# Decoder layer on one core: in the attention turns, two of four query products move ahead of the fourth tile's scores

## The chip, the cores and the metric

One core of a Trainium2 chip runs the whole program. The metric is the device time of one execution in microseconds (us); the median of three runs of the kernel before is 2265.24 us.

## The reference, cut to what matters

One decoder layer on x of shape (4, 2048, 512), in float32: a recurrent (S5) part, a cross attention and a feed-forward part, each behind a layer norm and added to x. The change touches only the stage of the cross attention:

```
x = x + S5(layernorm(x))
Q = layernorm(x) @ Wq.T            16 heads of 32; K, V from a context of 77 rows per batch
attn = softmax(Q K^T / sqrt(32))
x = x + (attn V) @ Wo.T
x = x + FFN(layernorm(x))
```

## The kernel before, in words

The program is written by hand, engine by engine: each engine has its own list of instructions, in order, and semaphores tie the lists together. The 8192 tokens are 16 groups (`NG`) of 512, each of `T` = 4 tiles of 128 tokens. The stage of the cross attention is a software pipeline of 18 turns (`attn_loop`, L419). Each engine has one body, called once a turn: `attn_pe` (L1925, TensorE), `attn_act` (L1052, ScalarE), `attn_dve` (L1440, VectorE) and `norm` (L852, GpSimd). In turn g, `has(d)` asks whether group g+d exists. A turn works on the scores of group g, on the queries of group g+1, on the values and half of the projection of group g-1 and on the other half of the projection of group g-2; group g+2 gets its layer-norm statistics (`spread2`, L1350).

A tile t of group g goes this way. `scores(t)` (L1938) is 48 matmuls of 32 rows into PSUM banks 0 to 3, and sets `s_done`. `shift(t)` on VectorE (L1474) takes the maxima and subtracts one half of them. `exp(t)` on ScalarE (L1079) is eight exponentials with sums and one large one. `sums(t)` on VectorE (L1487) ends in the reciprocal `rinv`. `norm` on GpSimd multiplies it in (L866). `turn_p(t, d)` on TensorE (L1960) transposes the result, in three slots. Tiles 2 and 3 are transposed only in the next turn, as `turn_p(2, -1)` and `turn_p(3, -1)`.

TensorE's results other than scores go through PSUM banks 4 to 7, by numbered slots: 28 a turn, slot n in bank 4 + n % 4 (P_SLOT to Q_SLOT, from L345). A slot is written by TensorE, copied by ScalarE rounded to its high part (`hi_p`, `hi_x`, `hi_v`, `hi_q`; L1059), and VectorE then writes the low part (`lo_p`, `lo_x`, `lo_v`, `lo_q`; L1314); the slots of `project` are added to x by `residual` (L1468) on VectorE alone. `bank(n)` (L1928) waits for VectorE to have finished the slot four before, and `scores(0)` waits for all slots of the turn before, since it reads the queries that `lo_q(3)` ends. All products are done in three passes (high by high, high by low, low by high), in `split3` (L442). A query product (`query`) is 12 matmuls of 512 columns, four make the next group's queries, into slots 24 to 27. They are written to `qh` and `ql`, which `scores` of the present group reads: no copy may start before `scores(3)` is done.

The order of a steady turn on TensorE is: `turn_p(2, -1)`, `scores(0)`, `project(2, -2)`, `turn_p(3, -1)`, `project(3, -2)`, `scores(1)`, four `values` with `turn_x(0)` and `turn_x(1)` between, `turn_p(0, 0)`, `scores(2)`, `turn_x(2)`, `project(0, -1)`, `turn_x(3)`, `project(1, -1)`, `turn_p(1, 0)`, `scores(3)`, four query products (L2058, L2059).

VectorE and ScalarE also prepare the feed-forward weights inside the turns, one block n a turn: `mix_weights(n)` (VectorE, L1403), `high_weights(n)` (ScalarE, L1039, L1041), then `low_weights(n, 0)` and `low_weights(n, 1)` (VectorE, L1413). These go from one SBUF tile to another. The sync engine's queue stores the block and loads the next (`store_wc`, L634; `load_wc`, L625), and in turns 2 to 13 then stores and loads groups of x (`turn`, L620). It waits for `low_weights(14, 1)` and, after that, for the last query product of turn 14 before it loads the first two groups for the feed-forward part (`load_x2`, L660, L675), whose statistics VectorE takes in turn 15 (`spread3`) and turn 16.

Turn 1 differs: it mixes block 1 late (`mix_weights(1)`), `high_weights(1)` stands behind `hi_q(0)`, and all four statistics of `spread2` come between the query copies. Turn 15 has no queries. Turn 0 has a list of its own in each body and returns early.

Of the kernel before, what the change touches and what calls it, by code (L numbers as in the profile page):

```python
# [20 lines left out]
def decoder_layer(nc, x, ctxT, log_dt, log_re, lam_im, vt, vinv, wqT, wkT, wvT, woT, wexpT, bexp, upbias,  # L21
# [13 lines left out]
    KC = D // P  # L35
# [18 lines left out]
    T = GT // P  # L54
    NG = NB * S // GT
# [225 lines left out]
    with ExitStack() as ctx:  # L281
# [633 lines left out]
        def _(act):  # L915
# [123 lines left out]
            def high_weights(n):  # L1039
                act.wait_ge(wc_ready, n + 1)  # L1040
                A(wc_h[:, :, :], wc_s[:, :, :], ACT.Copy).then_inc(wc_hi, 1)  # L1041
# [10 lines left out]
            def attn_act(g, has):  # L1052
                his.start()
                def hi(out, n):
                    act.wait_ge(pe_slot, SLOTS * g + n + 1)
                    bank = ps[:, 4 + n % 4, :]
                    if len(out.shape) == 3:
                        bank = bank[0:out.shape[0]].rearrange("p (j n) -> p j n", j=4)
                    his.done(A(out, bank, ACT.Copy), hi_slot(g, n))  # L1059

                def hi_p(t, d, qs=range(3)):
                    if has(d):
                        for q in qs:
                            part = (pth[:, 0:KC], pth[:, KC:2 * KC], pt2[0:KT])[q]
                            hi(part[:, :, t * P:(t + 1) * P], P_SLOT[t] + q)

                def hi_x(c):
                    if has(1):
                        hi(xt2h[:, c, :], x_slot(g, c))

                def hi_v(f):
                    if has(-1):
                        hi(aoh[:, f, :], V_SLOT[f])

                def hi_q(o):
                    if has(1):
                        hi(qh[:, o, :], q_slot(g, o))

                def exp(t):  # L1079
                    if has(0):  # L1080
                        act.wait_ge(top_ready, T * g + t + 1)
                        for h in range(HB, HPC):
                            for f in range(KC):
                                at, j = h * KC + f, f * HPC + h
                                e = A(es[t % 2][:, f, h * L:(h + 1) * L], ps[:, h, f * LP:f * LP + L], ACT.Exp,  # L1085
                                      bias=rmax[:, t % 2, at:at + 1], accum_out=rsum[:, t % 2, j:j + 1])
                        e.then_inc(exp_ps, 1)
                        act.wait_ge(e_ready, T * g + t + 1)
                        e = es[t % 2][:, :, 0:HB * L]
                        A(e, e, ACT.Exp).then_inc(exp_done, 1)  # L1090

                if g == 0:
                    exp(0)
                    for c in range(KC):
                        hi_x(c)
                    exp(1)
                    act.wait_ge(upb_ready, 1)
                    for i, out in enumerate(stage_out):
                        act.wait_ge(out, stage_turns(PIECES, i))
                    act.wait_ge(p_zero, 1)  # L1100
                    hi_p(0, 0)
                    exp(2)
                    hi_q(0)
                    hi_q(1)
                    hi_p(1, 0)
                    exp(3)
                    hi_q(2)
                    hi_q(3)
                    return
                hi_p(2, -1)  # L1110
                if g == 1:
                    act.wait_ge(wo_loaded, 16)
                    A(woh[:, :, :], wo_raw[:, :, :], ACT.Copy).then_inc(wo_hi, 1)
                if g == NG:
                    apply3(0)
                    for i in range(4):
                        raw_x(0, i, i, FIRST_TURN[i])
                exp(0)
                hi_p(3, -1)
                if has(1):  # L1120
                    apply2(g + 1)
                if g == NG:
                    act.wait_ge(x2_stored, 16 * (NG - 2))
                    act.wait_ge(wc_stored, 32 * NG)
                    hi_x3(0, B11)
                hi_v(0)
                hi_x(0)
                if g == 1:
                    high_weights(0)
                if g == NG:  # L1130
                    apply3(1, 0, 2)
                exp(1)
                hi_v(1)
                hi_x(1)
                if g == NG:
                    apply3(1, 2, T)
                hi_v(2)
                hi_v(3)
                if g == NG:
                    hi_x3(0, B21)  # L1140
                    for i in range(4, 8):
                        raw_x(0, i, i - 4, FIRST_TURN[i])
                    load_table(ACT.Gelu)
                    for o in FIRST_ORDER[2:]:
                        hi_x3(0, o)
                hi_p(0, 0)
                hi_x(2)
                if 2 <= g < NG:
                    high_weights(g)
                exp(2)  # L1150
                hi_x(3)
                hi_p(1, 0)
                exp(3)
                for o in range(KC):
                    hi_q(o)
                    if g == 1 and o == 0:
                        high_weights(1)

            attn_loop(act, attn_act)

            def gelu(p, c, q, i, chunk, src=None):
# [62 lines left out]
        def _(dve):  # L1224
# [125 lines left out]
            def spread2(g, tiles):  # L1350
                if tiles[0] == 0:
                    dve.wait_ge(x1_loaded, 16 * g + 16)
                ins = spread(x1[:, g % 4], tiles)
                if tiles[-1] == T - 1:
                    ins.then_inc(ln_step, 1)
# [84 lines left out]
            def attn_dve(g, has):  # L1440
# [8 lines left out]
                def lo_p(t, d):  # L1449
                    if has(d):  # L1450
                        for q, part, high in ((0, ptl[:, 0:KC], pth[:, 0:KC]), (1, ptl[:, KC:2 * KC], pth[:, KC:2 * KC]),
                                              (2, pt2[KB:KB + KT], pt2[0:KT])):
                            tok = slice(t * P, (t + 1) * P)
                            lo(part[:, :, tok], high[:, :, tok], P_SLOT[t] + q)
# [9 lines left out]
                def lo_q(o):  # L1464
                    if has(1):
                        lo(ql[:, o, :], qh[:, o, :], q_slot(g, o))
# [7 lines left out]
                def shift(t):  # L1474
                    if not has(0):
                        return
                    n = T * g + t
                    sc = ps[:, 0:HPC, 0:KC * LP].rearrange("p h (f k) -> p h f k", k=LP)[:, :, :, 0:L]
                    mx = rmax[:, t % 2, :].rearrange("p (h f) -> p h f", f=KC)
                    dve.wait_ge(s_done, n + 1)  # L1480
                    V.tensor_reduce(mx[:, HB:], sc[:, HB:], AX.X, ALU.max, negate=True).then_inc(top_ready, 1)  # L1481
                    V.tensor_reduce(mx[:, 0:HB], sc[:, 0:HB], AX.X, ALU.max).then_inc(max_step, 1)
                    dve.wait_ge(max_step, n + 1)
                    V.tensor_tensor(es[t % 2][:, :, 0:HB * L].rearrange("p f (h k) -> p h f k", k=L), sc[:, 0:HB],
                                    mx[:, 0:HB].unsqueeze(3).broadcast_to([P, HB, KC, L]), ALU.subtract).then_inc(e_ready, 1)
# [99 lines left out]
                if g == NG - 1:  # L1585
                    shift(3)
                lo_p(1, 0)
                if not (g == NG - 1):
                    shift(3)
                if g == 1:  # L1590
                    mix_weights(g)
                if has(2) and g > 1:
                    spread2(g + 2, range(0, 3))
                lo_q(0)
                if 0 <= g < NG - 1:
                    low_weights(g, 0)
                sums(3)
                if 0 <= g < NG - 1:
                    low_weights(g, 1)
                lo_q(1)  # L1600
                if has(2):
                    spread2(g + 2, range(3 if g > 1 else 0, T))
                lo_q(2)
                lo_q(3)

            attn_loop(dve, attn_dve)

# [145 lines left out]
        def _(pe):  # L1753
# [171 lines left out]
            def attn_pe(g, has):  # L1925
# [77 lines left out]
                def turn_q(os):  # L2003
                    if has(1):
                        pe.wait_ge(dve_slot, SLOTS * g + x_slot(g, 3) + 1)
                        for o in os:
                            slots.done(query(bank(q_slot(g, o)), o), q_slot(g, o))
# [47 lines left out]
                turn_x(3)  # L2055
                project(1, -1)
                turn_p(1, 0)
                scores(3)  # L2058
                turn_q(range(KC))  # L2059

            attn_loop(pe, attn_pe)

# [151 lines left out]
```

## Time and profile before

| what | value |
|---|---|
| runs | 2263.72, 2265.24, 2268.49 us; median 2265.24 |
| the profiled execution | 2265.3 us, its span on the core 2263.5 us |
| busy, share of the span | PE 98%, DVE 75%, ACT 54%, POOL 21% |
| attention turns 1 to 15 | from 297 us to about 945 us of the span |
| one steady turn | 43.66 us (562.70 to 606.36, start of `scores(0)`) |

PE is TensorE, PEld its weight loads, DVE VectorE, ACT ScalarE, POOL GpSimd, SPq the queue of the sync engine. Times in rows are microseconds from the span's start. An engine starts its next instruction some 0.1 us before the printed end of the last, so work in a row is best counted from start to start.

### The profile page before, as it was taken

Reading aid. Unit: us, or ns where it says so; the run is one execution under the profiler, and the core shown is the slowest. Engines: PE = TensorE matmul, PEld = TensorE weight load, DVE = VectorE, ACT = ScalarE, POOL = GpSimd, SP = SyncE. Lnnn points to the kernel's source line nnn. Section 1 sums busy time; section 2 is a strip of 40 time slices with the busy share of each in tenths; the row PEclk is TensorE's granted clock in tenths of the full one; section 3 lists DMA queues with packets and bytes.
Section 4 is the critical chain, followed back from the end, with each engine's and each line's share of the span. In section 5 each row is a group of like instructions: output and inputs, shape, how many; then the busy total and the mean of one; then the engine's idle time right before and its main releaser. Section 6 shows DMA issues by size and latency. Waiting matters only on the chain.

```text
span 2263.5 us, 41277 instructions
## 1 busy us (share of the span) xinstructions
PE 2218.5 (98%) x15960; PEld 1943.2 (86%) x15960; DVE 1701.5 (75%) x2854; ACT 1231.5 (54%) x2735; POOL 467.4 (21%) x578
## 2 busy tenths in 40 slices
PE   8899889999999999999999999999999999999999
PEld 7678777888888888778989989989989989889899
DVE  6666688888888888857947858758769668579467
ACT  3556566666766666645535536446446356355343
POOL 3531222322223222300020200300300300300203
PEclk8999999999999999999999999999999999999999
DMA  9999613323332331466676686786676676766765
GB/s 319 329 320 319 226 66 122 124 86 112 109 110 86 117 124 62 146 238 206 212 263 184 215 269 174 220 268 195 204 267 208 211 245 207 240 214 209 229 188 194
DMA packets 202091, 443.35 MB, mean 196 GB/s; under 512 B 32442, under 2 KB 70586, under 8 KB 200362
## 3 DMA queue, kind: packets, MB, share of 16 engines
q1 hardware_dynamic: 201898, 440.72, 60.2%
q8 instruction: 128, 2.10, 0.4%
q14 instruction: 65, 0.53, 0.1%
HBM read 341.66 MB, written 99.01 MB: 195 GB/s over the span
## 4 chain that ended last, share of the span: by engine, by line
PE 87%; ACT 5%; DVE 5%; DMA 2%; issue 1%; SPq 0%; POOL 0%; DVEq 0%; POOLq 0%; ACTq 0%
PE ps L442 69%; PE ps L1989 5%; PE ps L1957 4%; PE ps L1968 2%; ACT es L1085 2%; DMA yg<-in_wcon 1%; PE ps L1920 1%; PE ps L1877 1%; ACT wc_h L1041 1%; PE ps L1808 1%; DMA x_scratch<-xa 1%; PE ps L1859 1%; DVE rsum L1492 1%; ACT es L1090 1%; PE ps L1872 1%
## 5 line engine op out<-in xcount | busy, mean ns | idle before, releaser
L442 PE MATMUL ps<-ring,gh 128*128 128x256 f32 x3584 | 652.8, 284 | 0.1
L442 PEld LDWEIGHTS ps<-ring,gh 128*128 128x128 f32 x3584 | 558.2, 192 | 2.1 <-DVE gl L1314 1.5
L442 PE MATMUL ps<-xth,ring 128*128 128x512 f32 x1792 | 553.1, 389 | 0.0
L442 PE MATMUL ps<-ring,gl 128*128 128x256 f32 x1792 | 506.8, 283 | 0.0
L442 PEld LDWEIGHTS ps<-xth,ring 128*128 128x128 f32 x1792 | 336.4, 188 | 69.7
L1182 ACT ACTIVATE gh<-G 128x512 fp32r<-128x512 f32 x384 | 239.2, 629 | 218.6 <-PE ps L442 218.2
L442 PE MATMUL ps<-xtl,ring 128*128 128x512 f32 x896 | 348.6, 389 | 0.0
L442 PEld LDWEIGHTS ps<-ring,gl 128*128 128x128 f32 x1792 | 343.5, 192 | 0.0
L1314 DVE TENSOR_TENSOR gl<-G,gh 128x512 fp32r<-128x512 f32 x384 | 276.5, 732 | 51.4 <-ACT gh L1182 50.3
L866 POOL TENSOR_TENSOR es<-es,rinv 128x308 f32<-128x308 f32 x256 | 180.5, 736 | 388.8 <-DVE rinv L1496 388.8
L1165 ACT ACTIVATE G<-G,up_b 128x512 f32<-128x512 f32 x192 | 138.9, 723 | 222.0 <-DVE G L1608 222.0
L1608 DVE TENSOR_TENSOR U<-ps,U 128x512 f32<-128x512 f32 (+1 forms) x167 | 136.2, 815 | 163.4 <-PE ps L442 160.8
L1608 DVE TENSOR_TENSOR G<-ps,U 128x512 f32<-128x512 f32 x192 | 132.8, 692 | 113.9 <-PE ps L442 112.3
L756 POOL TENSOR_TENSOR rstd<-var_e,mhalf 128x4 f32<-128x4 f32 x48 | 50.5, 1051 | 745.5 <-DVE var_e L1295 745.5
L442 PEld LDWEIGHTS ps<-xtl,ring 128*128 128x128 f32 x896 | 168.2, 188 | 34.6
L1085 ACT ACTIVATE es<-ps,rmax 128x77 f32<-128x77 f32 x512 | 158.3, 341 | 69.6 <-DVE rmax L1481 69.6
L895 POOL TENSOR_TENSOR X<-X,U 128x256 f32<-128x256 f32 x64 | 72.2, 1158 | 472.7 <-DVE U L1608 472.7
L1165 ACT ACTIVATE G<-ps,up_b 128x512 f32<-128x512 f32 x64 | 44.2, 690 | 135.9 <-PE ps L442 135.9
L1085 ACT ACTIVATION_READ_ACCUMULATOR es<-ps,rmax 128x1 f32 x512 | 113.8, 222 | 0.0
L884 POOL TENSOR_TENSOR X<-X,ob 128x512 f32<-128x512 f32 x64 | 86.4, 1382 | 126.6 <-DMA X<-x_scratch 112.8
L442 PE MATMUL ps<-woh,aoh 128*128 128x512 f32 x256 | 106.9, 418 | 2.4 <-DVE x L1472 1.4
L1968 PE MATMUL ps<-ident,es 128*128 128x128 f32 (+1 forms) x768 | 99.2, 276 | 6.7 <-DVE xt2l L1314 2.2
(234 smaller groups left out, 4394.0 us busy)
## 6 DMA issues: line engine op xcount, KB each, us to landing
ring<-wup_scratch SPq DMA_DIRECT2D x224, 512.0 KB, 3.8
ring<-wdn_scratch SPq DMA_DIRECT2D x224, 512.0 KB, 3.6
X<-x_scratch SPq DMA_DIRECT2D x32, 1024.0 KB, 9.0
xa<-in_x SPq DMA_DIRECT2D x16, 1024.0 KB, 6.6
x_scratch<-xa SPq DMA_DIRECT2D x16, 1024.0 KB, 10.6
x<-x_scratch SPq DMA_DIRECT2D x16, 1024.0 KB, 5.6
x_scratch<-x SPq DMA_DIRECT2D x16, 1024.0 KB, 4.3
out_x<-X SPq DMA_DIRECT2D x15, 1024.0 KB, 6.4
```

Of the source, the lines that this page charges most:

```text
L442: mm = pe.matmul(bank, a, b, start=first and i == 0, stop=last and i == n - 1, skip_group_check=go_on)
L866: mul = nc.gpsimd.tensor_tensor(e[:, f], e[:, f], r[:, f].unsqueeze(2).broadcast_to([P, HPC, L]), ALU.mult)
L884: x = tt(X[:, i * T + t, :], X[:, i * T + t, :], ob[:, :], ALU.add)
L895: ins = tt(x, x, U[:, u + t // 2, t % 2 * HW:(t % 2 + 1) * HW], ALU.add)
L1085: e = A(es[t % 2][:, f, h * L:(h + 1) * L], ps[:, h, f * LP:f * LP + L], ACT.Exp, bias=rmax[:, t % 2, at:at + 1], accum_out=rsum[:, t % 2, ...
L1165: A(dst, dst if src is None else src, ACT.Gelu, bias=up_b[:, chunk:chunk + 1]).then_inc(gelu_done, 1)
L1182: A(gh[e % GR][:, :], src, ACT.Copy).then_inc(g_hi, 1)
L1314: sub = lambda o, a, b: V.tensor_tensor(o, a, b.bitcast(F32), ALU.subtract)
L1608: add = lambda o, a, b: V.tensor_tensor(o, a, b, ALU.add)
L1957: mm = pe.matmul(ps[:, h, cols], q[at, f, tok], k[at, b, f, :], start=(i == 0), stop=(i == 2))
L1968: mm = pe.transpose(b[0:keys.shape[1], j * P:(j + 1) * P], keys, ident[:, :])
L1989: mm = pe.matmul(b[0:VW[c]], v[:, f, V_AT[c]:V_AT[c + 1]], pt, start=(i == 0), stop=(i == len(passes) - 1))
```

## The change

On TensorE, query products 0 and 1 stand ahead of `scores(3)`, products 2 and 3 behind it. ScalarE waits for `scores(3)` to be done, copies queries 0 and 1, and only then does `exp(3)`; in turn 1, `high_weights(1)` comes before `hi_q(2)`. VectorE takes three statistics ahead of `shift(3)`, and `sums(3)` goes from behind `lo_q(0)` to behind `lo_q(3)`; the two parts of `low_weights` are spaced out between the query copies, and in turn 1 go to the very end.

```
@@ attn_act
                 exp(2)
                 hi_x(3)
                 hi_p(1, 0)
+                if has(1):
+                    act.wait_ge(s_done, T * g + T)
+                hi_q(0)
+                hi_q(1)
                 exp(3)
-                for o in range(KC):
-                    hi_q(o)
-                    if g == 1 and o == 0:
-                        high_weights(1)
+                if g == 1:
+                    high_weights(1)
+                hi_q(2)
+                hi_q(3)
@@ attn_dve
                 lo_p(1, 0)
+                if has(2) and g > 1:
+                    spread2(g + 2, range(0, 3))
                 if not (g == NG - 1):
                     shift(3)
+                lo_q(0)
+                lo_q(1)
                 if g == 1:
                     mix_weights(g)
-                if has(2) and g > 1:
-                    spread2(g + 2, range(0, 3))
-                lo_q(0)
-                if 0 <= g < NG - 1:
+                if 2 <= g < NG - 1:
                     low_weights(g, 0)
-                sums(3)
-                if 0 <= g < NG - 1:
+                lo_q(2)
+                if 2 <= g < NG - 1:
                     low_weights(g, 1)
-                lo_q(1)
                 if has(2):
                     spread2(g + 2, range(3 if g > 1 else 0, T))
-                lo_q(2)
                 lo_q(3)
+                sums(3)
+                if g == 1:
+                    low_weights(g, 0)
+                    low_weights(g, 1)
@@ attn_pe
                 turn_p(1, 0)
+                turn_q(range(2))
                 scores(3)
-                turn_q(range(KC))
+                turn_q(range(2, KC))
```

## Rows read from the trace of the kernel before

**Rows 1.** Chain of waits, 590 to 640 us: start, length, what.
```profile
592.38 1.47 PE ps L1957 x48
593.85 11.11 PE ps L442 x48
...
610.86 1.31 PE ps L1968 x12
```
**Rows 2.** Weight loads of TensorE in time, 590 to 616 us.
```profile
591.75 0.36 PEld L1968 LDWEIGHTS ps<-ident,es 128*66 128x66 f32 x4 [0.41 <-DVE xt2l L1314]
...
612.12 0.19 PEld L442 LDWEIGHTS ps<-woh,aoh 128*128 128x128 f32 x1 [0.22 <-DVE x L1472]
```
**Rows 3.** VectorE in order of time, a steady turn's end and the next one's start.
```profile
591.62 0.67 DVE L1472 TENSOR_TENSOR x<-x,ps 128x512 f32<-128x512 f32 x1
...
594.24 0.80 DVE L1481 TENSOR_REDUCE rmax<-ps 128x8 f32<-128x616 f32 x1
...
596.49 1.87 DVE L1277 BATCH_NORM_STATS2 st<-x 128x6 f32<-128x512 f32 x3
...
599.38 1.22 DVE L1314 TENSOR_TENSOR wc_s<-wc_s,wc_h 128x1024 f32<-128x1024 f32 x1
600.51 0.79 DVE L1492 TENSOR_REDUCE rsum<-es 128x8 f32<-128x616 f32 x1
...
601.50 0.90 DVE L1314 TENSOR_TENSOR wc_s<-wc_s,wc_h 128x768 f32<-128x768 f32 x1
...
605.62 0.69 DVE L1314 TENSOR_TENSOR ql<-ps,qh 128x512 fp32r<-128x512 f32 x1 [1.43 <-ACT qh L1059]
606.22 1.28 DVE L1314 TENSOR_TENSOR ptl<-ps,pth 128x512 fp32r<-128x512 f32 x2
...
611.39 0.68 DVE L1472 TENSOR_TENSOR x<-x,ps 128x512 f32<-128x512 f32 x1
```
**Rows 4.** ScalarE in order of time, the same stretch.
```profile
595.07 0.33 ACT L1085 ACTIVATE es<-ps,rmax 128x77 f32<-128x77 f32 x1 [2.06 <-DVE rmax L1481]
...
597.49 0.76 ACT L1090 ACTIVATE es<-es 128x616 f32<-128x616 f32 x1
...
605.48 1.08 ACT L1059 ACTIVATE pth<-ps 128x512 fp32r<-128x512 f32 x2
```
**Rows 5.** VectorE in order of time, turn 1 and the start of turn 2.
```profile
330.90 0.80 DVE L1481 TENSOR_REDUCE rmax<-ps 128x8 f32<-128x616 f32 x1
...
333.16 1.67 DVE L1405 TENSOR_TENSOR wc_s<-wc_s 128x256 f32<-128x256 f32 x4
...
340.57 2.46 DVE L1277 BATCH_NORM_STATS2 st<-x 128x6 f32<-128x512 f32 x4
...
349.31 0.68 DVE L1472 TENSOR_TENSOR x<-x,ps 128x512 f32<-128x512 f32 x1
```
**Rows 6.** ScalarE in order of time, turn 1.
```profile
335.25 1.75 ACT L1041 ACTIVATE wc_h<-wc_s 128x1792 fp32r<-128x1792 f32 x1
```
**Rows 7.** VectorE and GpSimd in order of time, the middle of turn 1.
```profile
318.30 2.45 DVE L1314 TENSOR_TENSOR wc_s<-wc_s,wc_h 128x1024 f32<-128x1024 f32 x2
...
316.13 2.67 POOL L866 TENSOR_TENSOR es<-es,rinv 128x308 f32<-128x308 f32 x4 [6.79 <-DVE rinv L1496]
```
**Rows 8.** Turns 14 and 15 in order of time: the sync queue, VectorE, TensorE.
```profile
908.28 0.56 SPq L640 DMA_DIRECT2D wdn_scratch<-wc_h  x1
...
910.78 1.78 SPq L661 DMA_DIRECT2D X<-x_scratch  x2
...
920.61 2.47 DVE L1277 BATCH_NORM_STATS2 st<-X 128x6 f32<-128x512 f32 x4
...
927.51 0.50 PE L1989 MATMUL ps<-pth,vh 128*128 128x512 f32 x1 [1.45 <-DVE aol L1314]
```
**Rows 9.** Busy time of the engines by stretches, then the granted clock, DMA share, GB/s.
```profile
295.90:299.30 3.40, 2.32 (x56) 2.27 (x57) 3.34 (x7) 1.37 (x1) 0.00 (x0) 1.00 0.00 0
299.40:302.70 3.30, 3.30 (x18) 3.18 (x16) 2.57 (x10) 2.99 (x17) 0.42 (x1) 0.50 0.00 0
```

## The prediction

> **What bounds the kernel now.** I read four views in this order. The page first: TensorE is busy for 98% of the span, so whatever delays it costs time, and work taken off another engine gives nothing by itself. Then the chain of waits through a steady turn of the attention stage, for the points at which TensorE is not its own bound. Nearly all of the chain is matmuls. The query products end at 593.85 + 11.11 = 604.96 [rows 1], 1.3 us of transposes follow, and the next turn's scores start at 606.36 after a wait of about 0.1 for the last query's copies. Third, the weight loads: the last transposes of `turn_p(1, 0)` wait 0.41 us for `xt2l`, and before `project(3)` at 612.12 TensorE waits 0.22 us for VectorE's residual L1472 [rows 2]. So VectorE's list from the end of one turn to that residual is level with TensorE: the residual ends at 611.39 + 0.68 = 612.07, and TensorE's transposes at 610.86 + 1.31 = 612.17 [rows 1, 3]. Fourth, VectorE in order of time, for where it has slack ahead of that point. It has little, a wait of 1.43 us for the last query's high part at 605.62 [rows 3].
>
> **A steady turn (2 to 13, twelve of them).** I lay the new lists end to end, with every duration from the rows.
>
> TensorE. Nothing changes up to the end of `turn_p(1, 0)`, where `scores(3)` starts at 592.38 [rows 1]. Now query 0 starts there. Its bank is free when the residual ends, 591.62 + 0.67 = 592.29 [rows 3], so that costs nothing, with a margin of 0.1. Two of four products take half of 11.11, 5.6 us, and then the scores 1.47 [rows 1]: `scores(3)` ends at 599.45 where it ended at 593.85. TensorE's own work until the next `project(3)` stays the same in sum.
>
> ScalarE. From 599.5 it copies queries 0 and 1 (0.5 each from start to start, half of 1.08), then the eight exponentials (595.07 to 597.49, 2.42) and the large one (0.7), then query 2 (0.6) [rows 4]: 4.7 us, so its high part is there at 604.2. Query 3 leaves TensorE at 605.0 as before.
>
> VectorE. The three statistics move ahead of `shift(3)`, from 594.2 to 596.1, into time in which it now waits for the scores; they cost nothing. What follows the scores, from start to start [rows 3]: `shift(3)` 2.25 (594.24 to 596.49); four `lo_q` at 0.6 (605.62 to 606.22), 2.4; `low_weights` 1.13 (599.38 to 600.51) and 0.8; one statistic 0.6 (a third of 1.87); `sums(3)` 1.0 (600.51 to 601.50). That is 8.2 us. Query 2's high part is ready just as VectorE comes to it (599.6 + 2.25 + 1.2 + 1.13 = 604.2), so ScalarE adds nothing. Starting at 599.6, VectorE reaches `lo_p(2)` of the next turn at 607.8, where it was at 606.22: **1.6 us late**. There is no more slack up to the residual (606.22 to 611.39, all of it `lo_p`, `shift(0)` and small steps that keep their order), so `project(3)` starts at 613.8 and not 612.1. All of this turn's `lo_q(3)` lateness, 0.6, lies inside the 1.6: `scores(0)` starts at 606.95. GpSimd gets `rinv` at 607.85 and takes 2.7 us [rows 7], done by 610.6; TensorE comes to `turn_p(3)` at 611.3, so `sums(3)` as such is not waited for. Behind `project(3)` everything hangs on TensorE or on VectorE's same list and moves rigidly. The sync queue stores the weight block some 3 us later in the turn and loads the next one later; that load is used by `mix_weights`, 14 us after the next `lo_p(2)`, and is taken as hidden. If that cover were gone, `mix_weights` would be late next, and `lo_v(1)` behind it.
>
> Twelve turns by 1.6 give **+19**.
>
> **Turn 1.** `shift(3)` started at 330.90 [rows 5], 0.4 behind its scores, since `lo_p` stood ahead of it; with 5.6 us of queries before them these scores now end at 336.1. From there: `shift(3)` 2.25, two `lo_q` 1.2, `mix_weights` 1.9 (four in 1.67, and one small) [rows 5], then ScalarE's `high_weights(1)` 1.6 [rows 6], which now stands before `hi_q(2)`, that copy 0.6, `lo_q(2)` 0.65, four statistics 2.4 [rows 5], `lo_q(3)` 0.6, `sums(3)` 1.0, `low_weights` 1.9: 14.1. So `lo_p(2)` starts near 350.3 and the residual, 5.2 later, near 355.4, where it was at 349.31 [rows 3, 5]: +6.1. To this comes a contention. The same two `low_weights` took 2.45 in the middle of the turn, where they began inside a run of GpSimd's (316.13 to 318.80) [rows 7], against 1.9 alone [rows 3]. In the new order they follow `rinv(3)` and so meet the run of GpSimd's again: +0.4. **Turn 1: +6.5.** The Trainium skill, "SBUF — State Buffer", section "Who interferes with whom", says that a VectorE instruction with two SBUF inputs and a GpSimd instruction that reads SBUF exclude each other, and that the one which comes second blocks for the whole instruction; by that rule up to a full GpSimd instruction (0.67, a quarter of 2.67) is lost in place of 0.4, and TensorE's `turn_p(3)` would see `norm` finish a whole `low_weights` later. The row of 2.45 agrees with it in kind.
>
> **Turns 14 and 15.** The second `low_weights` of turn 14 ends 6.1 us after the scores of tile 3 (2.25 + 1.2 + 1.13 + 0.6 + 0.9), which end at 905.2, 5.6 ahead of the last query's 910.78 [rows 8]: 911.4. Now the stores start there and not at 908.28, and the loads of X, which sit behind them in the queue, at 912.6 and not 910.78 [rows 8]. The first statistics of X started at 920.61 [rows 8] with, by my reading, half a microsecond to spare on the load. Two bounds: the issue is late by 1.9 and the stores ahead of it by 3.1, so the statistics are late by 1.4 to 2.6, and by 1.1 from VectorE's own list. I take 2.5, since the same 3.9 MB have to pass in the same order. The statistics delay the values behind them: at 927.51 TensorE had waited 1.45 for `aol` [rows 8], and that gap grows to 4. After gaps of that kind the clock has fallen: 2.32 us of busy TensorE in 3.40 is followed by a stretch at 0.50 [rows 9], the 1.2 GHz level. A stretch of 3.3 us at half rate loses 1.7 us of work. **Together +4.2.** Turn 0 and turn 15's own list are not changed.
>
> **The sum.** The profiled execution took 2265.3 us, level with the median of 2265.24. 2265.3 + 19.2 + 6.5 + 4.2 = **2295 us**.
>
> **Rivals.**
> *Only the scores wait.* If VectorE found a microsecond that I do not see before the residual, what is left is `lo_q(3)` at 0.6 a turn: 12 x 0.6, turn 1 at 4, turn 15 at 3: 2279 us. For it: TensorE needs only the query copies at the turn's start. Against it: the wait of 0.22 for the residual [rows 2] says that there is no such microsecond.
> *The clock falls in the steady turns too.* The stretch of transposes, a gap of 0.65 and 1.5 us of scores gets longer than before, and another gap of 1.6 comes at `project(3)`. A comparable stretch of 32-row scores, transposes and gaps was followed by half rate [rows 9]. Each case costs up to 1.7 where TensorE is the bound; half of the turns give +10 (2305), all +20 (2315). Against it: the wait at `project(3)` covers what is lost ahead of it. The Trainium skill, "TensorE: Matmul & The Clock Gate", section "Why this matters for your kernels", warns of gaps between bursts of matmuls for the same reason.
> *Faster.* The waits at the turn's two seams go: 0.4 before the last transposes of `turn_p(1)` and 0.2 at `project(3)` [rows 2]. The copies of queries 0 and 1 are done long before the turn's end, so a turn could lose 0.6: 14 x 0.6 gives 2257. It needs VectorE at `lo_p(2)` before 606.2, with 1.6 us less work behind the scores than I count; that is the point from which it decides. The first wait also comes from work that keeps its order.
> *No difference.* VectorE had waited 1.43 us in this stretch [rows 3]; if that takes up all, the turn stays: 2265. The 8.2 us count against it.
>
> **How the numbers follow.** Forecast 0.66; only the scores 0.13; clock 0.12; faster 0.04; none 0.05. About 0.2% (4.5 us) is what a measurement of this kernel can tell from no change. The forecast's own range is a turn's 1.6 within 0.4 (5 us), turn 1 within 1.5 and turn 15 within 2.5: 2287 to 2303. To hold 8 in 10 it is widened a little to both neighbours, 2282 to 2305. Faster 0.04, same 0.05, slower 0.91.
>
> **What would show it.** In the changed profile a steady turn lasts 45.2 us from `scores(0)` to `scores(0)`; the weight load of `project(3)` waits over 1 us for L1472; VectorE has idle time before `shift(3)` (about 3.4 us) and none from there to the residual; `scores(0)` waits some 0.7 for `lo_q(3)`; turn 1 is 6 to 7 us longer; the statistics of X in turn 15 start 2.5 us later against their scores. It is wrong if the residual's wait stays at 0.2, if VectorE still idles behind `shift(3)`, or if the granted clock of a steady turn falls under 1.00.

## The result, and the profile after

The changed kernel takes 2298.53 us (median of four runs, 2296.36 to 2301.37) against 2265.24: the ratio is 1.0143, 95% interval 1.0131 to 1.0156. It is 33 us slower. 2295 was forecast.

The profiled execution took 2301.4 us, span 2299.6. The page's first part and, below it, the chain of waits through the end of a steady turn (start, length, what):

```profile
span 2299.6 us, 41305 instructions
...
PE 2232.5 (97%) x15960; PEld 1949.3 (85%) x15960; DVE 1701.4 (74%) x2854; ACT 1228.2 (53%) x2735; POOL 461.3 (20%) x578
...
PE 81%; DVE 9%; ACT 4%; DMA 3%; issue 1%; SPq 0%; POOL 0%; DVEq 0%; POOLq 0%; ACTq 0%
```
```profile
612.72 5.72 PE ps L442 x24
618.44 1.47 PE ps L1964 x48
619.90 5.69 PE ps L442 x24
625.59 0.02 issue
625.61 0.60 ACT qh L1059
...
626.71 0.67 DVE ql L1318
627.38 0.71 DVE rsum L1496
...
628.37 1.14 DVE ptl L1318 x2
...
630.25 0.80 DVE rmax L1485
...
633.48 0.60 DVE x L1476
634.08 0.04 issue
634.12 3.02 PE ps L442 x12
```

The work is the same: as many matmuls, and VectorE busy for the same 1701 us. In the kernel before the chain leaves the query products at 604.96 [rows 1] and is back on TensorE at 606.36. Here the chain leaves TensorE at 625.6 and comes back only at 634.12, by way of ScalarE's last query copy and then VectorE's list in its own order: last query's low part, sums, `lo_p(2)`, `shift(0)`, moments, residual. VectorE's share of the chain goes from 5% to 9%.

VectorE in order of time shows why, and where it was free just before:

```profile
614.51 1.88 DVE L1281 BATCH_NORM_STATS2 st<-x 128x6 f32<-128x512 f32 x3
619.96 0.80 DVE L1485 TENSOR_REDUCE rmax<-ps 128x8 f32<-128x616 f32 x1 [3.57 <-PE ps L1964]
...
622.22 1.28 DVE L1318 TENSOR_TENSOR ql<-ps,qh 128x512 fp32r<-128x512 f32 x2
623.41 1.22 DVE L1318 TENSOR_TENSOR wc_s<-wc_s,wc_h 128x1024 f32<-128x1024 f32 x1
624.63 0.69 DVE L1318 TENSOR_TENSOR ql<-ps,qh 128x512 fp32r<-128x512 f32 x1
625.24 0.95 DVE L1318 TENSOR_TENSOR wc_s<-wc_s,wc_h 128x768 f32<-128x768 f32 x1
626.10 0.68 DVE L1281 BATCH_NORM_STATS2 st<-x 128x6 f32<-128x512 f32 x1
626.71 0.67 DVE L1318 TENSOR_TENSOR ql<-ps,qh 128x512 fp32r<-128x512 f32 x1
627.30 0.78 DVE L1496 TENSOR_REDUCE rsum<-es 128x8 f32<-128x616 f32 x1
...
628.28 1.22 DVE L1318 TENSOR_TENSOR ptl<-ps,pth 128x512 fp32r<-128x512 f32 x2
...
633.39 0.68 DVE L1476 TENSOR_TENSOR x<-x,ps 128x512 f32<-128x512 f32 x1
```

It idles 3.57 us for the scores of tile 3, which TensorE now ends 5.6 us later, and then has no gap any more: from 619.96 to `lo_p(2)` at 628.28 it works 8.3 us without a break, where it had waited 1.43 us in the same stretch [rows 3]. Two waits on TensorE are the result (weight loads in order of time, the wait before them in brackets):

```profile
627.43 0.19 PEld L1964 LDWEIGHTS ps<-kh,qh 32*128 32x128 f32 x4 [0.81 <-DVE ql L1318]
...
634.12 0.19 PEld L442 LDWEIGHTS ps<-woh,aoh 128*128 128x128 f32 x1 [1.17 <-DVE x L1476]
```

In the kernel before, the waits at the same two places were 0.37 and 0.22, the second in [rows 2].

**Where the 36 us of the two profiled executions lie.** Measured from `scores(0)` to `scores(0)`, from the starts of L1957 and L1964 matmuls:

| stretch | before | after | difference |
|---|---|---|---|
| start to turn 1 | 296.98 | 302.06 | +5.1 |
| turn 1 | 47.29 | 50.53 | +3.2 |
| turn 2 | 43.70 | 47.90 | +4.2 |
| turns 3 to 13, each | 43.67 to 43.71 | 45.37 to 45.41 | +1.70, eleven times: +18.7 |
| turn 14 | 43.67 | 44.92 | +1.3 |
| turn 15 to the end | 1351.3 | 1355.0 | +3.6 |

The 5.1 us ahead of turn 1, where nothing that the change touches runs, are scatter: the experiments below reach turn 1 between 295.7 and 302.0 us. Without them 31 us are left. `scores(0)` does not yet show all of a turn's delay, since the wait at `project(3)` follows. Counted up to `project(3)` of turn 2, turn 1 costs 361.78 - 350.05 - 5.08 = 6.65 us. From there to `project(3)` of turn 14, twelve turns by 1.70 add 20.4, and the rest of the program adds 3.9.

The start of turn 2 also ran at half clock, behind waits of 2.04 and 2.60 us at the weight loads of its first transposes and of `scores(0)`. The row is turn 2 of the changed kernel (span, busy times of PE, PEld, DVE, ACT and POOL, then granted clock, DMA share, GB/s):

```profile
352.60:400.40 47.80, 46.78 (x384) 38.00 (x384) 39.93 (x69) 28.81 (x97) 13.47 (x18) 0.93 0.29 96
```

The half clock lasts from 352.3 to 359.1. It cost nothing at `project(3)`: VectorE worked without a gap through it, and the weight load there still waited 0.64 us for the residual.

### The profile page after: what moved, and what is told of

Its sections match the earlier page's. It is cut to its first block, busy times and chain, and to the rows that moved or that the text cites. A ratio compares the mean times of both kernels' runs of the same rounds, so it can differ in the third digit from the quotient of the medians.

```text
span 2299.6 us, 41305 instructions
## 1 busy us (share of the span) xinstructions
PE 2232.5 (97%) x15960; PEld 1949.3 (85%) x15960; DVE 1701.4 (74%) x2854; ACT 1228.2 (53%) x2735; POOL 461.3 (20%) x578
## 4 chain that ended last, share of the span: by engine, by line
PE 81%; DVE 9%; ACT 4%; DMA 3%; issue 1%; SPq 0%; POOL 0%; DVEq 0%; POOLq 0%; ACTq 0%
PE ps L442 65%; PE ps L1996 5%; PE ps L1964 3%; ACT es L1085 2%; PE ps L1975 2%; DMA x_scratch<-xa 1%; PE ps L1927 1%; PE ps L1884 1%; DVE ql L1318 1%; ACT wc_h L1041 1%; PE ps L1815 1%; DVE rsum L1496 1%; DVE rmax L1485 1%; DVE ptl L1318 1%; DVE wc_s L1318 1%
## 5 line engine op out<-in xcount | busy, mean ns | idle before, releaser
L866 POOL TENSOR_TENSOR es<-es,rinv 128x308 f32<-128x308 f32 x256 | 173.9, 710 | 478.2 <-DVE rinv L1500 478.2
L442 PE MATMUL ps<-xt2h,wqh 128*128 128x512 f32 x256 | 103.3, 404 | 3.5 <-DVE pt L1318 2.8
## 6 DMA issues: line engine op xcount, KB each, us to landing
x_scratch<-xa SPq DMA_DIRECT2D x16, 1024.0 KB, 10.7
```

What stands on the lines that cost most here:

```text
L442: mm = pe.matmul(bank, a, b, start=first and i == 0, stop=last and i == n - 1, skip_group_check=go_on)
L866: mul = nc.gpsimd.tensor_tensor(e[:, f], e[:, f], r[:, f].unsqueeze(2).broadcast_to([P, HPC, L]), ALU.mult)
```

## The experiments

The theory: what costs is the length of VectorE's list between the scores of tile 3 and the residual before `project(3)`. VectorE was level with TensorE there, and the change makes it start 5.6 us later, with 1.9 us of it moved ahead only. The rivals: the late softmax sums, the split of the query products itself (its banks, ScalarE's wait), or the clock. Each kernel ran on a chip together with the kernel before, which measured 2265.6 to 2267.2 us in the three sessions.

**1. The sums early.** Edit of the changed kernel:

```
                 if 2 <= g < NG - 1:
                     low_weights(g, 0)
+                sums(3)
                 lo_q(2)
...
                 lo_q(3)
-                sums(3)
```


> Changed kernel, with sums(3) moved from behind lo_q(3) to before lo_q(2) (turns 1 to 15). Theory (what costs is the length of VectorE's list between the scores of tile 3 and the residual before project(3), in whatever order): the list is as long as before, so a steady turn stays at 45.4 us, scores(0) waits some 1 us longer and project(3) 1 us less, total 2298 to 2300. Rival (what costs is that the softmax sums now end late, so that GpSimd and turn_p(3) are late): a turn falls to about 44.4, total 2286.

Measured: 2305.52 us, ratio 1.0171 (1.0156 to 1.0186), where 2298 to 2300 was expected. The rival falls: nothing is gained. But the steady turns took 45.43 to 45.49 and 46.80 to 46.83 us in alternation up to turn 12, and turn 13 was long as well. The first number is the theory's, the second was a surprise. The weight load of one `scores(0)`, and two windows of a long turn (span, busy times, then granted clock):

```profile
577.80 0.19 PEld L1964 LDWEIGHTS ps<-kh,qh 32*128 32x128 f32 x4 [1.83 <-DVE ql L1318]
```
```profile
621.20:625.00 3.80, 2.23 (x54) 1.92 (x52) 3.77 (x6) 1.24 (x3) 2.67 (x3) 1.00 0.54 182
625.20:628.50 3.30, 3.30 (x10) 2.56 (x9) 3.02 (x10) 2.54 (x17) 0.00 (x0) 0.50 0.96 325
```

The wait at `scores(0)` has grown from 0.81 to 1.8, and in each of the six long turns (4, 6, 8, 10, 12, 13) the stretch behind it runs at half clock, 1.2 GHz. There `project(2)` took 4.45 us and not 2.85. Experiments 7 and 8 test that.

**2. The weights early.** Both `low_weights` of turns 2 to 14 go into the idle time:

```
                     spread2(g + 2, range(0, 3))
+                if 2 <= g < NG - 1:
+                    low_weights(g, 0)
+                    low_weights(g, 1)
                 if not (g == NG - 1):
                     shift(3)
...
-                if 2 <= g < NG - 1:
-                    low_weights(g, 0)
                 lo_q(2)
-                if 2 <= g < NG - 1:
-                    low_weights(g, 1)
```


> Changed kernel, with both low_weights of turns 2 to 14 moved ahead of shift(3), into the time in which VectorE waits for the scores. Theory: 1.9 us leave the list behind the scores, but lo_q(3) can't start before its high part is there, so only 0.7 a turn come back: a steady turn 44.7, the X loads of turn 15 are issued on time again (-3), total about 2286. Rival (the split of the query products itself, its ScalarE wait or its banks, costs the 1.7): a turn stays at 45.4, total 2295.

Measured: 2289.74 us, 1.0097 (1.0080 to 1.0114); a steady turn 44.94 us. Part of it came back, as the theory has it: 1.9 us of work left the list and 0.45 us a turn were gained, since `lo_q(3)` then waits for its high part. 0.7 a turn and 2286 in all were expected. Behind `scores(0)` of turn 15 another 3.6 us came back, for the reason that experiment 9 tests. Totals have to be read with care: turn 1, whose instructions are those of the changed kernel, took 49.09 us here and 50.53 there, with one stretch at half clock early in it in place of two.

**3. The list short.** As 2, with all four statistics ahead of `shift(3)` and `sums(3)` before `lo_q(2)`:

```
-                    spread2(g + 2, range(0, 3))
+                    spread2(g + 2, range(T))
...
+                sums(3)
                 lo_q(2)
-                if has(2):
-                    spread2(g + 2, range(3 if g > 1 else 0, T))
+                if has(2) and g == 1:
+                    spread2(g + 2, range(T))
                 lo_q(3)
-                sums(3)
```


> Changed kernel, with low_weights and all four statistics of turns 2 to 14 ahead of shift(3), and sums(3) before lo_q(2). Theory: lo_q(3) is then bound by the query copy alone, as in the kernel before, and lo_p(2) starts where it did: a steady turn 43.8, total about 2274 (turn 1 still carries its 5 to 6 us). Rival (split of the products): over 45, total over 2292.

Measured: 2273.25 us, 1.0032 (1.0020 to 1.0044), a steady turn 44.0 us. TensorE's order and ScalarE's are those of the changed kernel, word for word, and 25 of the 33 us are gone. In the profiled executions turns 3 to 13 give back 15.1 us, and the part from `scores(0)` of turn 15 on gives back 3.5. VectorE in order of time:

```profile
599.46 2.47 DVE L1281 BATCH_NORM_STATS2 st<-x 128x6 f32<-128x512 f32 x4
601.85 2.08 DVE L1318 TENSOR_TENSOR wc_s<-wc_s,wc_h 128x1024 f32<-128x1024 f32 x2
604.86 0.80 DVE L1485 TENSOR_REDUCE rmax<-ps 128x8 f32<-128x616 f32 x1 [0.94 <-PE ps L1963]
...
609.04 0.79 DVE L1496 TENSOR_REDUCE rsum<-es 128x8 f32<-128x616 f32 x1 [0.65 <-ACT es L1090]
...
611.15 0.69 DVE L1318 TENSOR_TENSOR ql<-ps,qh 128x512 fp32r<-128x512 f32 x1 [0.48 <-ACT qh L1059]
611.76 1.28 DVE L1318 TENSOR_TENSOR ptl<-ps,pth 128x512 fp32r<-128x512 f32 x2
```

`lo_p(2)` starts 6.9 us after `shift(3)`, no longer 8.3, and now with waits of 0.65 and 0.48 in it. 0.3 us a turn are left (44.0 against 43.67) for the split of the products and for all else in which the lists still differ; about 0.1 of it shows at query 0, whose weight load waits 0.28 us for the residual of `project(1)`.

**4. Turn 1 in its old order.** `scores(3)` ahead of all products, `exp(3)` ahead of the copies, and VectorE's list of the kernel before, for `g == 1` alone, on all three engines; on TensorE:

```
+                if g == 1:
+                    scores(3)
+                    turn_q(range(KC))
+                    return
                 turn_q(range(2))
```


> Changed kernel, with turn 1 in the order of the kernel before on all three engines. Theory: turn 1 alone gives back its 6.5 us, steady turns stay at 45.4: total 2292. Rival (the steady turns carry it all, turn 1's delay is absorbed later): total 2298.

Measured: 2291.79 us, 1.0111 (1.0096 to 1.0126): 6.7 us less than the changed kernel, 6.5 expected. Turn 1 lasts 47.30 us again, the steady turns (3 to 13) stay at 45.33 to 45.42.

**5 and 6. One more statistic.** A single additional `bn_stats` on VectorE, in turns 2 to 13, ahead of `shift(3)` and then behind the second `low_weights`:

```
+                if has(2) and g > 1:
+                    spread(x1[:, (g + 2) % 4], range(3, 4))
                 if not (g == NG - 1):
                     shift(3)
```


> Changed kernel, with one more statistic (0.6 us of VectorE, its result is written again later) ahead of shift(3) in turns 2 to 13, where VectorE waits for the scores. Theory: nothing changes, a steady turn stays at 45.4. Rival (VectorE is short of time anywhere in the turn): 46.0.

Measured, one run: 2299.94 us, a steady turn 45.36 (45.33 to 45.40).

```
                     low_weights(g, 1)
+                if has(2) and g > 1:
+                    spread(x1[:, (g + 2) % 4], range(0, 1))
                 if has(2):
```


> The same additional statistic (0.6 us) behind the second low_weights, that is behind the scores. Theory: every turn pays it in full, a steady turn 46.0, total some 7 us more than the changed kernel; if the gap at scores(0), then 1.3 us, sets off the clock as in s1, every second turn more. Rival (there is slack for it): 45.4.

Measured, one run: 2309.8 us. A steady turn takes 45.94 to 46.00, and 46.34 to 46.40 in turns 3, 7, 11 and 13, each with a stretch at half clock behind a wait of 1.4 us at `scores(0)`. The same 0.6 us cost nothing on one side of `shift(3)` and 0.6 us a turn on the other. That is the theory in one pair of runs; each is a single run, and it is the turns of its trace, which agree among themselves, that carry the reading. The half clock costs only 0.4 us a turn here: in these four turns the wait for the residual at `project(3)`, 1.17 otherwise, is gone and has covered the rest. In experiment 1 that wait was down to 0.23, and a stretch at half clock cost 1.36.

**7 and 8. Keeping the clock.** Small matmuls on TensorE inside its wait at `scores(0)`, in the kernel of experiment 1. Their result is overwritten by the scores:

```
                 turn_p(2, -1)
+                if 2 <= g < NG:
+                    pe.wait_ge(e_ready, T * g)
+                    pe.wait_ge(exp_ps, T * g)
+                    keep_clock(0, 16)
                 scores(0)
```


> s1_sums_early with 16 small matmuls (128 x 128, into a free bank, their result is overwritten) on TensorE ahead of scores(0) in turns 2 to 15, inside its wait there. In s1 every second steady turn took 46.8 us and not 45.5, with a stretch at half clock behind the wait at scores(0). Theory (the 1.4 us are the clock's, set off by the longer idle stretch): all steady turns take 45.4 to 45.5, total about 2297. Rival (the alternation comes from a DMA or a semaphore): it stays, total 2305.

Measured: 2316.28 us, 1.0225 (1.0212 to 1.0238), where 2297 was expected. The turns no longer alternate and the clock stays full, but each takes 47.2 us: the 16 matmuls came to 32 in the trace and 3.67 us, past the release. With 7:

> As s1_keep_clock, with 7 matmuls in the source and not 16. There each one became two of about 0.11 us, 3.67 us in all, so they held TensorE beyond VectorE's release; now they take 1.6 us of a wait of 1.75. Theory (clock): full clock in all steady turns and 45.4 to 45.5 each, total about 2298. Rival: the turns of 46.8 stay, total 2305.

Measured: 2297.06 us, 1.0134 (1.0114 to 1.0154). All steady turns take 45.44 to 45.50. The filler and a window over turns 2 and 3:

```profile
624.47 1.73 PE L2018 MATMUL ps<-ident 128*128 128x128 f32 x14
```
```profile
349.00:440.00 91.00, 87.82 (x779) 71.65 (x778) 75.30 (x132) 56.42 (x191) 21.91 (x33) 1.00 0.30 100
```

So the 1.4 us of the long turns in experiment 1 were the clock's. With them taken out a steady turn is within 0.1 us of the changed kernel's 45.39: the order of the sums by itself gives nothing. That the total of 2297 also meets the 2298 expected is in part luck. The filler stands in turn 15 as well; there no half clock followed the gap in the values, and from `scores(0)` of turn 15 to the end it took 1351.8 us, against 1355.0 in the changed kernel.

**9. Turn 14's weights early.** As experiment 2, for `g == NG - 2` alone:

```
                     spread2(g + 2, range(0, 3))
+                if g == NG - 2:
+                    low_weights(g, 0)
+                    low_weights(g, 1)
...
-                if 2 <= g < NG - 1:
+                if 2 <= g < NG - 2:
```


> Changed kernel, with the two low_weights of turn 14 alone moved ahead of shift(3). Theory (the stores of weight block 14, late behind low_weights, hold back the two loads of X for the statistics of turn 15): the loads are issued with the last query product again, the statistics start some 2 us earlier, and TensorE's gap in the values of turn 15 closes to about 1.6 us; total 2298.5 - 3.5 = 2295. Rival (the statistics are late from VectorE's own list): not over 1 us gained.

Measured: 2292.86 us, 1.0118 (1.0105 to 1.0131), 5.7 us less than the changed kernel, where 3.5 was expected; from `scores(0)` of turn 15 to the end the profiled executions differ by 3.6 (1351.4 against 1355.0), and that is the part that the theory speaks of. The other 2 us are within the spread of the runs. The changed kernel's queue, statistics and values (timelines of the sync queue, VectorE, TensorE):

```profile
943.90 0.56 SPq L640 DMA_DIRECT2D wdn_scratch<-wc_h  x1
...
945.21 2.90 SPq L661 DMA_DIRECT2D X<-x_scratch  x2
...
955.33 2.47 DVE L1281 BATCH_NORM_STATS2 st<-X 128x6 f32<-128x512 f32 x4 [1.36 <-DMA X<-x_scratch]
...
962.22 0.50 PE L1996 MATMUL ps<-pth,vh 128*128 128x512 f32 x1 [3.43 <-DVE aol L1318]
```

and in experiment 9:

```profile
937.87 0.92 SPq L661 DMA_DIRECT2D X<-x_scratch  x2
...
948.62 2.47 DVE L1281 BATCH_NORM_STATS2 st<-X 128x6 f32<-128x512 f32 x4
...
955.52 0.50 PE L1999 MATMUL ps<-pth,vh 128*128 128x512 f32 x1 [2.08 <-DVE aol L1318]
```

The two executions are to be compared from `scores(0)` of turn 15, at 944.62 and 939.25. The issue moves from +0.6 to -1.4 us, the statistics from +10.7 to +9.4; they were at +8.45 in the kernel before, and the last microsecond is VectorE's own list. The wait for the DMA is gone. The gap in the values is 2.08 and not 3.43 (1.6 was expected), and the half clock that followed it is gone. A second stretch at half clock, 36 us into turn 15 of the changed kernel, is absent here too, but it is not what costs: experiments 2 and 3 have one there, of 3.4 and 6.8 us, and end with the same 1351.4.

**10 and 11. What can be had, in either order.** In the new order, with the short list of experiment 3:

```
@@ attn_act
-                if 2 <= g < NG:
+                if g == NG - 1:
                     high_weights(g)
                 exp(2)
                 hi_x(3)
                 hi_p(1, 0)
+                if 1 <= g < NG - 1:
+                    high_weights(g)
@@ attn_dve
+                residual(2, -2)
                 if has(1) and g > 1:
                     moments2(g + 1)
-                residual(2, -2)
```

In turn 1 the statistics and `mix_weights(1)` go ahead of `shift(3)`, and `low_weights(1, 0)` and `(1, 1)` between its query copies.

> The new order of TensorE with VectorE's short list (as s3), and besides: high_weights of turns 1 to 14 goes from ahead of exp(2) to behind hi_p(1, 0) on ScalarE, where ScalarE now waits for scores(3); the residual before project(3) goes ahead of the layer-norm moments on VectorE; in turn 1 the statistics and mix_weights go ahead of shift(3). Theory (TensorE waits only at the seams that VectorE's and ScalarE's lists make): the wait of 0.4 before the last transposes of turn_p(1) and the waits of 0.1 to 0.3 at query 0 and project(3) go, a steady turn is 43.2 to 43.4, turn 1 within 2 us of the kernel before: total 2259 to 2263. Rival (the split of the products has a cost of its own of 0.3 us a turn or more): a turn of 43.7 or more, total 2267 or more.

Measured: 2256.81 us (2254.73 to 2262.56), 0.9964 (0.9951 to 0.9976), 2 us under the range expected; a steady turn (3 to 14) 43.12 to 43.18, turn 1 46.42 and turn 2, with a stretch at half clock, 44.74.

The kernel before with the same two edits (`high_weights` of turns 2 to 14) and nothing else:

> The kernel before, in its old order of TensorE, with only two moves: high_weights of turns 2 to 14 behind hi_p(1, 0), and the residual before project(3) ahead of the moments. Theory: the same two waits go (0.4 and 0.2 a turn), a steady turn of 43.1 to 43.3, total 2258 to 2261. If it is as fast as c_best_new_order or faster, the order of the products gives nothing. Rival (exp(3) is pushed late by high_weights and takes the gain back): 43.7, total 2265.

Measured: 2258.32 us (2254.81 to 2262.53), 0.9966 (0.9954 to 0.9979); a steady turn 43.06 to 43.14. Both beat the kernel before, by 0.3% to 0.4%, and they don't differ from each other by anything the runs can tell. Their steady turns differ by 0.06 us, and so the split of the products, once VectorE's list is short, costs next to nothing and gains nothing. In the steady turns of experiment 10 TensorE is busy for nearly the whole time (550 us within turns 2 to 14, in the column order of the windows above):

```profile
350.00:900.00 550.00, 548.75 (x4855) 452.09 (x4854) 481.25 (x840) 372.82 (x1233) 152.17 (x230) 1.00 0.32 106
```

## Why the prediction was right, point by point

**The steady turn.** 1.6 us late was forecast and 1.70 measured, 45.39 us where 45.2 was named. The list came to 8.3 and not 8.2 us. Another tenth is at query 0. The prediction took the bank as free when TensorE came to it, with a margin of 0.1. But its weight load waited 0.29 us for the residual of `project(1)`, at 612.68, just ahead of the matmul at 612.72, and the stretch from the start of these transposes to the product behind them grew from 1.76 to 1.87 us. Twelve turns by 0.1 are 1.2 of the missing microseconds. The signs that the prediction named are there: 3.57 us idle before `shift(3)` for 3.4, no gap behind it, 0.81 at `scores(0)` for 0.7, 1.17 at `project(3)` for over 1. Experiments 3, 5 and 6 show that the mechanism is this one, and not only that the sum came out.

**The sums and GpSimd.** They were forecast as not waited for. Experiment 1 with the clock kept (8) puts them early again, and a steady turn is 45.44 to 45.50 us, not shorter than the changed kernel's.

**Turn 1.** +6.5 forecast, +6.65 in the trace, 6.7 by experiment 4. That it is met so closely is in part luck: both profiled executions had two stretches at half clock early in turn 1, and the same turn with one such stretch was 1.4 us shorter (experiment 2). Its terms are to be seen, too: VectorE waits 2.25 us for the query copy behind `high_weights(1)`, and the two `low_weights` meet GpSimd's run again (VectorE, then GpSimd, in order of time).

```profile
348.88 0.69 DVE L1318 TENSOR_TENSOR ql<-ps,qh 128x512 fp32r<-128x512 f32 x1 [2.25 <-ACT qh L1059]
...
353.44 2.53 DVE L1318 TENSOR_TENSOR wc_s<-wc_s,wc_h 128x1024 f32<-128x1024 f32 x2
```
```profile
353.60 4.24 POOL L866 TENSOR_TENSOR es<-es,rinv 128x308 f32<-128x308 f32 x4 [18.06 <-DVE rinv L1500]
```

Together they take 2.53 us, some 0.5 more than the 2.08 that experiment 3 shows for the same pair with GpSimd idle, and GpSimd's four take 4.24 and not 2.67 [rows 7]. The Trainium skill, "SBUF — State Buffer", section "Who interferes with whom", has them exclude each other for whole instructions; the 0.4 of the forecast from the row and the 0.67 by the rule have the 0.5 between them. GpSimd's loss (1.6 us) is the larger one. It is not waited for here.

**Turns 14 and 15.** +4.2 forecast, +3.9 measured, both counted from `project(3)` of turn 14, up to which the twelve turns by 1.6 reach. There the changed execution was 906.40 - 874.26 = 32.14 us behind. The first late matmul of the values stands 962.22 - 927.51 = 34.71 behind: +2.6 where 2.5 was taken. (0.6 of it is there at `project(3)` of turn 15.) The statistics of X are 2.6 late on the same count, and 2.3 against the scores of turn 15, where the list of signs has 2.5. Behind the gap the clock was at half, and sixteen matmuls took 5.37 us where 3.79 had been: +1.6 where 1.7 was taken. Some 0.3 of these 4.2 us are gained again before the end; where is not known.

**The rivals.** *Only the scores wait* and *no difference* fell with the 1.17 us at `project(3)`. *The clock in the steady turns* did not come in turns 3 to 14, which have full clock throughout. It did come in turn 2, which the prediction counts among the steady ones, and a granted clock under 1.00 in one of them was named as a sign of being wrong. The argument that the prediction set against this rival held there: the wait for the residual covered the loss. But the rival was nearer than its chance of 0.12 said. 0.6 us more of wait at `scores(0)` (experiment 6) brings the half clock in four turns of turns 3 to 13, a whole microsecond more (experiment 1) in six. *Faster* needed 1.6 us less work behind the scores. Experiment 3 brings `lo_p(2)` forward by 1.4 against `shift(3)` and is still 0.3% slower than the kernel before; it takes the two moves of experiment 10 to turn the sign, and these work as well without the change. The wait of 0.4 before the last transposes, which the prediction called one that keeps, is gone in both of these, in experiment 11 without any change in the order of the products. Which of their two moves removes it was not tested apart; that it is `high_weights`, which stood ahead of the copies that these transposes wait for, is argued only.

**The sum.** Steady turns 20.4 (12 by 1.70) for 19.2, turn 1 6.65 for 6.5, turns 14 and 15 3.9 for 4.2: 31 for 29.9. The medians differ by 33, 2 us above that; the runs of either kernel spread over 5 us, no run tells where these 2 us lie, and the forecast range of 2282 to 2305 held them. The narrower range that the prediction names, 2287 to 2303, is a little tighter than its own terms: 5, 1.5 and 2.5 make 9 us to each side.

## What to carry to other kernels

Where two engines are level, an order that makes one of them start late has to be costed on its whole list from the late start to the next place where it is waited for: 0.6 us in front of the late point were free, the same 0.6 us behind it cost 0.6 us a turn. Moving products ahead of the scores on the busiest engine gave nothing by itself here; what gave 0.3% was to place the side work of the other engines (here weight preparation) where they wait anyway, and to let the work that somebody waits for go ahead of the work that nobody does. A DMA issue that sits in a queue behind a semaphore wait moves with the last instruction that this wait names, and so with work that has nothing to do with it.

## What the runs showed of the hardware that was not expected

The granted clock fell to half after waits that did not idle TensorE for long. In experiment 1, a wait of 1.8 us between transposes and the 32-row score matmuls was followed by half clock in six of turns 3 to 13 (five of them at intervals of 92 us), in experiment 6 a wait of 1.4 us in four of them; with 0.81 us, in the changed kernel, it never was. 1.7 us of 128 x 128 matmuls inside the wait removed it, and turns 3 to 13 took 8.0 us less together (500.2 for 508.2). The Trainium skill, "TensorE: Matmul & The Clock Gate", section "Why this matters for your kernels", warns of gaps between bursts of matmuls; here transposes and score matmuls around the gap did not save the clock, and what counts as enough of them stays open. Each filler matmul of float32 was recorded as two of about 0.12 us (14 in 1.73 us for 7 in the source), so a filler has to be sized from the trace.
